# Attention: two score banks instead of three in the first pass, two output banks instead of one

## The reference, cut to what matters

```
x = L0_attn_x
sa, ca, ga, sb, cb, gb = (mod[:, 0], ..., mod[:, 5])
h = _layernorm(x, axis=-1) * (1 + ca) + sa

q = (x @ Wq).reshape(Bsz, Tlen, H, D)
k = x @ Wk
v = x @ Wv
scores = jnp.einsum('bihd,bjd->bhij', q, k) / jnp.sqrt(jnp.float32(D))
scores = jnp.where(causal, scores, -jnp.inf)
attn = jax.nn.softmax(scores, axis=-1)
out = jnp.einsum('bhij,bjd->bihd', attn, v).reshape(Bsz, Tlen, C)
return out @ Wo + bo
```

## Time and profile before

| | us |
|---|---|
| median of 3 runs | 1195.96 |
| lowest and highest | 1193.53, 1196.80 |
| profiled execution | 1198.01 |
| its span in the trace | 1196.1 |
| TensorE busy, of the span | 979.8 (82%) |
| VectorE busy | 660.5 (55%) |
| ScalarE busy | 532.4 (45%) |
| granted TensorE clock, mean | 0.925 |

### The profile page before, as it was taken

The page is one execution under the profiler, slowest core; times in us unless marked ns, Lnnn a source line. Parts: engine busy times, 40 slices in busy tenths (PEclk is TensorE's granted clock), DMA queues, the critical chain, the costliest instruction groups (busy, mean ns, idle before and its releaser), DMA issues. The chain is left out here.

```text
span 1196.1 us, 24906 instructions
## 1 busy us (share of the span) xinstructions
PE 979.8 (82%) x9819; PEld 625.3 (52%) x9823; DVE 660.5 (55%) x1744; ACT 532.4 (45%) x827; POOL 305.7 (26%) x353
## 2 busy tenths in 40 slices
PE   4896899999999999965099999338467689999994
PEld 3433343344334455332067777213245689999994
DVE  4048989999999999226000000389775623333331
ACT  2524565566666777754022322154026443333330
POOL 2004411101001110110512222226820034455542
PEclk9998999999999999997589999759789799999998
DMA  6896003000000000009215554300036713223233
GB/s 207 141 152 144 3 2 4 2 3 2 3 2 2 3 3 2 1 2 338 86 30 164 116 166 100 81 1 1 0 101 232 230 41 47 46 47 48 49 48 88
DMA packets 73467, 81.90 MB, mean 68 GB/s; under 512 B 22928, under 2 KB 64528, under 8 KB 72672
## 3 DMA queue, kind: packets, MB, share of 16 engines
q1 hardware_dynamic: 58976, 61.45, 19.4%
q0 software_dynamic: 12288, 17.10, 8.5%
q10 hardware_dynamic: 2112, 2.10, 0.6%
HBM read 58.45 MB, written 24.13 MB: 69 GB/s over the span
## 5 line engine op out<-in xcount | busy, mean ns | idle before, releaser
L537 ACT ACTIVATE k_prob<-f_s 128x1024 f32<-128x1024 f32 (+3 forms) x320 | 270.3, 896 | 142.0 <-PE f_s L385 141.6
L593 DVE TENSOR_REDUCE k_mpart<-f_r 128x1 f32<-128x512 f32 x384 | 250.4, 684 | 11.3 <-PE f_r L342 9.5
L342 PE MATMUL f_r<-k_ks,k_qs 112*32 112x512 bf16 (+3 forms) x2560 | 210.1, 354 | 17.7 <-DVE k_mpart L593 10.3
L385 PE MATMUL f_s<-k_qs,k_ks 114*32 114x512 bf16 (+3 forms) x2560 | 175.3, 350 | 4.4 <-ACT k_prob L537 2.2
L401 PE MATMUL f_o<-k_prob,k_vaug 128*32 128x512 f32 (+3 forms) x1280 | 148.2, 532 | 4.2 <-issue 3.7
L342 PEld LDWEIGHTS f_r<-k_ks,k_qs 112*32 112x32 bf16 x2560 | 70.3, 95 | 143.3 <-DVE k_mpart L593 63.0
L779 POOL TENSOR_SCALAR_AFFINE_SELECT k_prob<-k_prob 128x256 f32<-128x256 f32 x128 | 52.2, 413 | 326.0 <-ACT k_prob L537 324.7
L590 DVE CUSTOM_DVE_ANT_0 k_unread<-f_r,k_causal 128x128 bf16<-128x128 f32 (+3 forms) x256 | 121.0, 484 | 22.4 <-PE f_r L342 21.0
L385 PEld LDWEIGHTS f_s<-k_qs,k_ks 114*32 114x32 bf16 x2560 | 65.9, 97 | 73.0 <-ACT k_prob L537 21.0
L1855 DVE TENSOR_TENSOR mid<-silu_g,e_u 128x512 f32<-128x512 f32 x39 | 26.8, 688 | 126.0 <-PE e_u L1760 126.0
L1354 DVE SCALAR_TENSOR_TENSOR outr<-p_o,rows,k_mod 128x256 f32<-128x256 f32 x16 | 7.7, 484 | 140.9 <-PE p_o L1311 140.9
(11 more groups left out here) (280 smaller groups left out, 1283.7 us busy)
## 6 DMA issues: line engine op xcount, KB each, us to landing
r_raw<-in_L_ffn_w_dram SPq DMA_DIRECT2D x24, 512.0 KB, 5.8
k_wi<-in_L_ffn_wi_dram SPq DMA_DIRECT2D x8, 1024.0 KB, 5.0
k_wo_e<-in_L_ffn_wo_dram SPq DMA_DIRECT2D x8, 1024.0 KB, 7.3
k_qs<-q_dram SPq DMA_DIRECT2D x21, 256.0 KB, 9.5
sum<-k_x SPq DMA_DIRECT2D x8, 512.0 KB, 6.9
q_dram<-k_q_parts SPq DMA_DIRECT2D x12, 256.0 KB, 12.0
disp<-k_wmod SPq DMA_DIRECT2D x2, 1310.0 KB, 6.4
rows<-disp SPq DMA_DIRECT2D x8, 262.0 KB, 2.7
```

Source lines behind the costliest of these rows:

```text
L342: last = nc.tensor.matmul(bank(r)[32 * j:32 * (j + 1), 0:w], qs[0:KROWS, c, GH * g + hs, q0:q0 + 32], ks[0:KROWS, QC * ck:QC * ck + w], st ...
L385: last = nc.tensor.matmul(sc[pair][32 * j:32 * (j + 1), i, off:QC], ks[0:KALL, k0:k0 + 32], qs[0:KALL, c, GH * g + 2 * pair + i, off:QC], ...
L537: nc.scalar.activation(prob[:, u % 2, 2 * pair:2 * pair + 2, off:QC], sc[pair][:, :, off:QC], ACT.Exp, scale=HD ** -0.5).then_inc(e_done, 1)
L593: nc.vector.reduce_max(mpart[:, s % 2, hs, t, ck:ck + 1], bank(r)[:, 0:w], AX.X).then_inc(ring_used[r % RING], 1)
```

## The change

The ring gets two banks instead of three, and the bank that this frees becomes a second output bank: group s uses output bank s mod 2, and its first values step waits for the copy of group s - 2 instead of s - 1. The projections and the modulation columns, which also used the output bank, use the first of the two. The list of entries and the order of every engine's instructions stay as they are.

```
-RING = 3
+RING = 2
...
-        ot = ctx.enter_context(nc.psum_tensor("f_o", [P, QC], FP))
-        pj = [sc[1][:, 0, :], sc[1][:, 1, :], ot[:, :]]
+        ots = [ctx.enter_context(nc.psum_tensor(f"f_o{s}", [P, QC], FP)) for s in range(2)]
+        pj = [sc[1][:, 0, :], sc[1][:, 1, :], ots[0][:, :]]
...
-                if kt == 0 and s:
-                    pe.wait_ge(o_copied, s)
+                if kt == 0 and s >= 2:
+                    pe.wait_ge(o_copied, s - 1)
                 for j in range(GH):
-                    last = nc.tensor.matmul(ot[32 * j:32 * (j + 1), off:QC], vaug[:, kt, :],
+                    last = nc.tensor.matmul(ots[s % 2][32 * j:32 * (j + 1), off:QC], vaug[:, kt, :],
...
-                nc.scalar.copy(oT[:, c % 2, g, :], ot[:, :]).then_inc(o_copied, 1)
+                nc.scalar.copy(oT[:, c % 2, g, :], ots[s % 2][:, :]).then_inc(o_copied, 1)
```

More of the change, by code:

```diff
@@ L410, in _ @@
                     for t in range(KH):
-                        last = nc.tensor.matmul(ot[:, 2 * m + half:2 * m + half + 1],
+                        last = nc.tensor.matmul(ots[0][:, 2 * m + half:2 * m + half + 1],
                                                 wmod[:, 0, t, D * m + P * half:D * m + P * (half + 1)],
@@ L634, in _ @@
             dve.wait_ge(col_done, 1)
-            nc.vector.tensor_copy(modcol[:, 0, :], ot[:, 0:KH]).then_inc(col_ready, 1)
-            nc.vector.tensor_scalar_add(modcol[:, 1, :], ot[:, KH:2 * KH], 1.0).then_inc(col_ready, 1)
+            nc.vector.tensor_copy(modcol[:, 0, :], ots[0][:, 0:KH]).then_inc(col_ready, 1)
+            nc.vector.tensor_scalar_add(modcol[:, 1, :], ots[0][:, KH:2 * KH], 1.0).then_inc(col_ready, 1)
             normal(1)
```

## The result

The changed kernel takes 1268.64 us (median of 4 runs, 1266.36 to 1272.26) against 1196.27 for the kernel before (4 runs): a ratio of 1.061, with a 95% interval of 1.058 to 1.064. It is 72 us slower. The forecast was 46 us slower with a range up to 1266: the direction is right, the size is too small, and the time lies above the range. The mechanism that was forecast is there, but it makes up only part of the loss.

A forecast was written before the change was run, and what follows sets the result against it. TensorE and VectorE, both 95% busy, were taken to be bound through the score ring between them, VectorE mostly setting the pace. 35 + 2 + 2 + 6 + 1 = +46 us on 1196 gave 1242 us, range 1218 to 1266.

The forecast's parts named there:

- The walk of one unit: Loop: the third chunk waits for the first one's reader, so a unit takes 2.84 us instead of 2.49, +0.35.
- A unit with five chunks adds one reader of 0.65 or less to before and after alike: Loop, five-chunk units: the fifth chunk costs the same before and after, so no loss beyond the gap at the values step.
- the two small terms for the units with a shorter V: Loop: values step of 384 columns, 13 units at 0.16, 2 us; still shorter, perhaps twenty units with narrow chunks, 2 us.
- The average of 0.37: Loop: 0.37 us charged to each of 95 units with a full-width values step, 35 us (24 to 48).
- The start: Stretch before the loop: six modulation pieces share the ring with chunks, each next piece 1.2 later, five times: 6 us (0 to 9).
- The walk between the modulation pieces: Before the loop: with two banks the next piece starts at 82.05 instead of 80.85, 1.2 us later, five times.
- The tail: Output steps of the last query block: transposes and projections wait for VectorE's normalisations, 1 us (0.3 to 3).
- The output bank at 0: Group starts: the second output bank gains 0, at most 9 us, as the copy ends 0.45 us before the values step.
- two banks do for the loop: Rival: a chunk's round trip of 0.53 is below the neighbour's 0.65 read, so only start and tail remain: 1203; chance 0.04.
- faster: Rival: the copy really holds the values step at group starts, so up to 9 us come back: 1187; chance 0.02.
- half: Rival: slack at group ends and in five-chunk units absorbs part, 0.20 a unit, start swallowed: 1219; chance 0.10.
- the clock falls too: Rival: TensorE's short pauses lower its granted clock to 0.9, 17 us more in the loop: 1259; chance 0.08.

The follow-up runs named there:

- e5: The changed kernel with the values step cut into two halves of 256 query columns, the third chunk between them: 1242.33 us, ratio 1.0388 to the kernel before.
- e7: The changed kernel with every chunk on the diagonal computed and read at the full 512 columns under a wider mask: 1287.27 us, ratio 1.0767 to the kernel before.
- e1: The kernel before with two ring banks for the first 50 ring entries only, three elsewhere, one output bank: 1206.21 us, ratio 1.0053.
- e10: The changed kernel measured and profiled once more, with no further edit: 1267.61 us, ratio 1.0580 to the kernel before.
- e4: The kernel before with two ring banks and nothing else, one output bank, a PSUM bank unused: 1270.05 us, ratio 1.0589.
- e2: The kernel before with two ring banks for the entries of the units only, three before and after, one output bank: 1258.48 us, ratio 1.0491.
- e8: The kernel before, three ring banks, with the diagonal chunks at the full 512 columns: 1229.31 us, ratio 1.0278.
- e9: The changed kernel with both the values step cut in two and all diagonal chunks 512 wide: 1257.43 us, ratio 1.0500 to the kernel before.

## Why the prediction fell short

**The walk of one unit was right.** In 55 units with V at full width, four chunks and nothing else, the distance from one V to the next grew from 2.51 to 2.85 us, +0.34, and the walk had given 0.34, 0.35 and 0.45. VectorE goes idle across V, as it had said. One of its readings was off without harm: the 0.39 us from P4 to its reader were not P4's way to VectorE but VectorE at work on P3 until 394.92; where VectorE stands for a chunk of 256 columns it is 0.33.

**The step that failed is "A unit with five chunks adds one reader of 0.65 or less to before and after alike", together with the two small terms for the units with a shorter V, 0.16 each at 384 columns and "up to 0.23, and 0.11, in perhaps twenty such units".** The average of 0.37 was taken from the plainest unit for all 95. The traces have, for the units with V at full width:

| units | how many | before | after | more |
|---|---|---|---|---|
| four chunks, no other entry | 55 | 2.51 | 2.85 | 0.34 |
| five chunks | 23 | 2.97 | 3.65 | 0.68 |
| four chunks and an A, B or C entry | 16 | 3.17 | 3.70 | 0.53 |

With two more, which have both five chunks and such an entry and lost 2.7 us, these 96 units lost 45.7 us, 0.48 each, where 0.37 was charged. The units of the first group shift against each other by up to 3.6 us, which sums to 0.2. Of the others 13 each have V at 384, 256 and 128 columns; they lost 5.1, 3.9 and 3.2 us, 12.2 in all, where 2 + 2 had been charged. So of the 19 us by which the loop's forecast of 39 was short, some 8 are these units' (12.2 - 4), 7 those with five chunks (23 x 0.31), and 4 to 5 those with A, B and C entries (16 x 0.16, and 2.0 for the two), less 2 where the plain units lost 0.34 instead of 0.37.

How a five-chunk unit loses twice is in the timeline of the changed kernel, from one V to the next (391.80 to 395.27, 3.47 us):

```profile
391.80 1.03 PE L401 MATMUL f_o<-k_prob,k_vaug 128*32 128x512 f32 x8
...
392.66 0.60 PE L342 MATMUL f_r<-k_ks,k_qs 112*32 112x512 bf16 x8
...
393.10 1.89 DVE L593 TENSOR_REDUCE k_mpart<-f_r 128x1 f32<-128x512 f32 x3 [0.33 <-PE f_r L342]
...
394.51 0.23 PE L342 MATMUL f_r<-k_ks,k_qs 112*32 112x128 bf16 x4
394.91 0.28 DVE L590 CUSTOM_DVE_ANT_0 k_unread<-f_r,k_causal 128x128 bf16<-128x128 f32 x1
...
395.05 0.40 PE L342 MATMUL f_r<-k_ks,k_qs 112*32 112x512 bf16 x4 [0.31 <-DVE k_mpart L593]
...
395.27 1.03 PE L401 MATMUL f_o<-k_prob,k_vaug 128*32 128x512 f32 x8
...
395.50 0.69 DVE L593 TENSOR_REDUCE k_mpart<-f_r 128x1 f32<-128x512 f32 x1 [0.30 <-PE f_r L342]
```

VectorE stood for 0.33 us at P4, which came behind V. Then the narrow chunk P2 (394.51) is read in 0.28, while P3 could start only at 395.05, when P1's bank was free, and needs 0.45 until VectorE can start on it: another 0.30. Before, P3 did not have to wait for P1's reader. The prediction had this arithmetic (a round trip of 0.53 against reads of 0.30 and 0.42), and then left it out wherever V is wide. They are two gaps at two places of the unit.

**VectorE's own books agree.** From ScalarE's first exponential of unit 0 to that of unit 140, VectorE's rows in the traces give, sorted by the chunk that it stood for:

| us | before | after | more | forecast |
|---|---|---|---|---|
| idle at P4, behind V | 6.3 | 34.7 | 28.4 | about 24 (95 x 0.25) |
| idle behind a chunk of 128 or 256 columns, elsewhere | 6.2 | 20.1 | 13.9 | 2 |
| all other idle time | 10.6 | 13.5 | 2.9 | 0 |
| overlap of a row with the one before it (less of it costs time) | 55.8 | 43.7 | 12.1 less | none named |
| lengths of all rows | 416.8 | 417.8 | 1.0 | 0 |

They sum to the loop's 58 us. The fourth line is a loss that shows as busy time: the page's sum for VectorE grew by 14.1 us (674.6 against 660.5), though the two kinds of reader took only 2.8 us more when each is taken by itself (251.8 + 122.4 against 250.4 + 121.0). Of the 600 reads of these units VectorE had gone idle at 101 before and at 243 after, and a read at which it has gone idle has no overlap with the last one. The walk did count some of it (it used 0.65 and 0.69 by place), but the bound of 0.25 at VectorE alone did not, and where the banks are full reads start 0.61 apart, not 0.65, which no term had. With V cut (e5) the idle time at P4 is back at 6.3 us and the narrow chunks' is still 22.1; with full widths (e7) it is the other way round, 35.8 and 3.2. The two are separate causes, each with its own experiment.

**The other terms.** The start was forecast at 6, and e1's 6.3 meets that partly by luck: its unit 0 is 8.8 us late, and the loop with three banks wins some of it back. With two banks in the loop nearly all of it stays (9.3 at unit 0 in e10, 8.6 in e4), at the edge of the bound of 9. The walk between the modulation pieces was right: they stand 4.29 us apart instead of 3.22 (84.20, 88.49, 92.78, 97.08 and 101.36 in the changed kernel), +1.07 where the walk gave 1.2, and from the first to the sixth e10 has 6.0 us more than before. What was not walked is the way to the first piece, 2.0 later in e10, and from the last one to unit 0, 1.3 longer. The tail is undersized, 2.3 to 2.5 us in the traces for a forecast of 1: the projections wait for normalisations that the transposes hold up, as this timeline of TensorE in the changed kernel shows, where the earlier trace rows had the first projection 0.67 after the third transpose and here it is 1.47 (597.82 - 596.35):

```profile
596.35 0.66 PE L351 MATMUL f_r<-k_ident,k_oT 128*128 128x128 f32 x4
...
597.82 1.13 PE L368 MATMUL f_r<-k_wo,k_wmod 128*128 128x256 f32 x4 [0.59 <-DVE k_wmod L607]
```

The output bank at 0 is right (e4). Of the rivals, "two banks do for the loop", "faster" and "half" are refuted by the result and by e2, and "the clock falls too" by the granted clock of 1.00 over 416 us. The Trainium skill describes a kernel whose clock swings between its two levels because TensorE idles for moments between matmul groups that cycle through PSUM banks ("TensorE: Matmul & The Clock Gate", A second HAM failure mode); here TensorE did so in every unit, busy for 88% of the time, and the trace does not agree: the granted clock stayed at 1.00.

**What stays open.** Cutting V gives back 23 to 27 us and the wide chunks 11 to 14, while both together leave about 26 of the 72. Of that remainder the traces of e8 and e9 place 6 us ahead of unit 0, 19 in the loop and 4 behind it. In the loop 8.5 us lie in the 24 units with A, B and C entries, 0.35 each, but no experiment took these entries out; and about half of the 19 is overlap between VectorE's rows, which is read from the traces and was not tested by an experiment of its own. The experiments settle that V and the narrow chunks are causes with these sizes; that the remainder belongs to two banks as such, whatever the order and the widths, is the reading that e9 leaves standing, and it is not shown. None of the kernels beats the one before.

## What to carry to other kernels

A ring between two engines that each work in program order needs so many banks that the filled ones keep the reader busy while the producer is away on its longest other step and then refills one: here V (0.86 us) and the 0.44 until a full chunk can be read, against what is left to read in two banks. That test must be made at each kind of unit, not at the plainest, since each irregular step (a chunk that is read faster, a fifth chunk, an entry with another reader) meets an empty ring again and pays its own round trip. A bank that a long step of the producer needs can be replaced by cutting that step in two, but only as far as that step is the cause: 23 to 27 of the 72 us here. Before a buffer is given away, look in the trace for who waits for the one that is to be doubled: here it was one instruction, 0.8 us in the whole run. And an engine without idle time is not yet at its fastest: look at how far apart its rows start (0.60 or 0.65 us here).

## What the runs showed of the hardware

VectorE's reductions of a PSUM bank over 512 columns last 0.68 to 0.69 us each, but where they follow each other directly and the banks are already full they start 0.60 to 0.61 us apart, and 0.65 where the next bank is filled only just in time (e8 and e9). A ring that runs dry loses the overlap each time, 12 us in the loop here (142 more reads at which it had gone idle), and it is booked as busy time. From the end of VectorE's read to TensorE's next weight load it is 0.06 us. From the first matmul of a chunk to the start of its reading, where VectorE stood idle for it, it is 0.31 us at 128 columns, 0.33 at 256, 0.39 at 384 and 0.44 at 512 (medians of the changed kernel; the kernel before has the same at 256 columns and more). TensorE at 88% busy, idle for about 0.34 us per unit on average, kept a granted clock of 1.00 throughout the 416 us.
